# A fused cross-attention kernel: the sum of squares folded over two partition halves, one matmul per norm, output products reordered

## The chip, the cores and the metric

The kernel runs on one core of one Trainium2 chip. Time is device time in microseconds of one execution; the profiled execution has its own time and, in its trace, a span from the first to the last instruction. TensorE (PE in the rows) multiplies, VectorE (DVE), ScalarE (ACT) and GpSimd (POOL) work elementwise, SyncE (SP) issues most of the DMAs. Each runs its instructions in order, and they wait for each other through semaphores.

## What is computed

One cross-attention layer over 64 sequences of 256 tokens, in float32. The text input x has 512 features, the context 384, the hidden size is 512. Cut to its core:

```python
text_p = einsum('bld,dh->blh', H_l, W_text) + b_text
audio_p = einsum('bsd,dh->bsh', H_a, W_audio) + b_audio
Q = layer_norm(text_p, g1, beta1)
K = layer_norm(audio_p, g2, beta2)
alpha = softmax(einsum('blh,bsh->bls', Q, K) / sqrt(512))
H_hyper = einsum('bls,bsh->blh', alpha, audio_p)
H_hyper = einsum('blh,hk->blk', H_hyper, W_out) + b_out
out = layer_norm(H_hyper + H_l, g_out, beta_out)
```

## The kernel before

**Steps.** A step handles two sequences, 512 tokens, and there are N = 32 of them. The first two and the last two are written out, the others run in a loop of two steps a turn (run_steps). In step i the projections, the norms and the scores of step i are made, together with the probabilities, the context product and the output product of step j = i - 1, and the last norm of the rows of step i - 2.

**Two-part numbers.** The operands of TensorE are written in type fp32r, in two parts: a high part, and a low part that holds what is left of the float32 value. Each product is three matmuls: high by high, high by low, low by high. The high part is a copy on ScalarE, as a rule, and the low part a subtraction on VectorE (low, shifted_low).

**K and Q.** project_k and project_q give four tiles each (h = 0 to 3) of 128 hidden features by 512 tokens, into the PSUM banks wide0 to wide3. The mean over the features is already taken out, through centred weights. k_centre and q_centre on ScalarE read a tile twice: its square goes to squares[:, h, :], the tile itself to k_cols or q_cols. The variance is the mean of squares over all 512 features: POOL adds tiles 0 and 1 (pair_squares), VectorE adds tile 2 (add_square) and tile 3 (sum_squares), splits the 128x512 sum into sq_hi and sq_lo (split_sum), and mean_squares on TensorE multiplies each by a constant 128x128 matrix of 1/512 (mean_of), two matmuls into one bank, turn0 for k and turn1 for q. The bank then holds the variance of each token in all 128 rows. rstd_of on ScalarE (Ln, then Exp) turns it into 1/sqrt in place, k_norm or q_norm on VectorE multiplies each tile by it, k_high or q_high on ScalarE and k_low or q_low on VectorE split the result. The scores need kT and qT in both parts. scores waits for one qT tile per term: qT_split counts them, and the first product, scores(0, 0), waits for all four, one before each term of three matmuls.

**The rest of a step.** turn_p turns the probabilities of step j with transposes of 32 rows on VectorE, sixteen a step (512 in all), twelve ahead of the k sum and four behind it. pT_high and pT_low split them. probs_context(j, d) makes the context product in three blocks d = 0, 1, 2 into score[0], score[1] and turn0; pc_high and pc_low split each, and output_part(j, t, d) multiplies block d with the folded output weights into wide[t]: three matmuls for each of four row tiles t and three blocks d, 36 a step. y_sum adds the rows, y_stat and y_moment give the statistics, scales on POOL the factors, y_norm on ScalarE normalises, and finish_y on POOL multiplies by go_row and adds betao_row (lines 963 and 965).

**What sets the order.** There is no scheduler. The order on each engine is the order of the calls in its step function. The ones that the change touches: on TensorE mean_squares(k) stands between project_q(1) and project_q(2), and mean_squares(q) between probs_context(j, 2) and the output products. On VectorE the k sum stands behind twelve transposes. On ScalarE q_centre(0) follows y_norm(i - 2, odd, 0); xT_high(i + 1), a 128x2048 copy, stands between q_high(1) and q_high(2).

Of the kernel before, what the change touches and what calls it, by code (L numbers as in the profile page):

```python
# [14 lines left out]
P = 128  # L15
# [3 lines left out]
def cross_attention_kernel(nc, x_rows, xT, c_rows, cT, w_text, b_text, w_audio, b_audio, w_out, b_out,  # L19
# [11 lines left out]
    with ExitStack() as stack:  # L31
# [39 lines left out]
        sq_hi, sq_lo = sb("sq_hi", [P, T * P], F32R), sb("sq_lo", [P, T * P], F32R)  # L71
# [51 lines left out]
        mean_of_made = sem("mean_of_made")  # L123
        k_log, q_log, k_rstd, q_rstd = sem("k_log"), sem("q_log"), sem("k_rstd"), sem("q_rstd")
# [7 lines left out]
        k_added, k_summed, k_sq_hi, k_sq_lo = sem("k_added"), sem("k_summed"), sem("k_sq_hi"), sem("k_sq_lo")  # L132
        q_added, q_summed, q_sq_hi, q_sq_lo = sem("q_added"), sem("q_summed"), sem("q_sq_hi"), sem("q_sq_lo")
# [117 lines left out]
        def _(pe):  # L251
# [48 lines left out]
            def mean_squares(i, to, sq_hi_made, sq_lo_made, var):  # L300

                pe.wait_ge(sq_hi_made, i + 1)
                nc.tensor.matmul(to, mean_of[:], sq_hi[:], start=True, stop=False)
                pe.wait_ge(sq_lo_made, i + 1)
                nc.tensor.matmul(to, mean_of[:], sq_lo[:], start=False, stop=True).then_inc(var, 1)  # L305
# [73 lines left out]
            def step(i, odd, first=False, last=False):  # L379
# [5 lines left out]
                mean_squares(i, turn[0][:], k_sq_hi, k_sq_lo, k_var)  # L385
# [12 lines left out]
                mean_squares(i, turn[1][:], q_sq_hi, q_sq_lo, q_var)  # L398
                if not first:

                    pe.wait_ge(q_centred, HT * i + 2)
                    output_part(j, 0, 0)
                    output_part(j, 0, 1)
                    output_part(j, 1, 0)
                if not first:
                    output_part(j, 0, 2)
                    output_part(j, 1, 1)
                    output_part(j, 1, 2)
                    for t in range(2, T - 1 if last else T):
                        pe.wait_ge(q_centred, HT * i + t + 1)  # L410
                        output(j, t)
# [26 lines left out]
        def _(act):  # L438
# [37 lines left out]
            def k_centre(i, h):  # L476
                wait(act, kT_split, HT * (i - 1) + h + 1)
                wait(act, q_sq_lo if h == 3 else q_summed, i)
                centre(k_cols, h, bac_col, k_done, i, k_centred, k_squared)

            def q_centre(i, h):
                wait(act, qT_split, HT * (i - 1) + h + 1)
                act.wait_ge(k_sq_lo if h == 3 else k_summed, i + 1)
                centre(q_cols, h, btc_col, q_done, i, q_centred, q_squared)

# [62 lines left out]
            def step(i, odd, first=False, last=False):  # L548
# [13 lines left out]
                k_centre(i, 3)  # L562
                if late:
                    y_norm(i - 2, odd, 0)
# [11 lines left out]
                q_centre(i, 3)  # L576
                k_high(i, 3)
# [3 lines left out]
                else:  # L581
                    for d in range(CT):
# [491 lines left out]
```

## Time and profile before

| what | value |
|---|---|
| median of 3 runs | 1299.43 us (1299.04 to 1299.71) |
| profiled execution: its time | 1299.89 us |
| its span | 1298.1 us |
| mean granted TensorE clock | 0.992 of full speed |
| TensorE busy | 98% |
| VectorE busy | 1164.0 us, 90% |
| ScalarE busy | 1001.5 us, 77% |
| POOL busy | 724.4 us, 56% |

Busy shares are of the whole span. A matmul is listed with its own time from start to drained result (395 ns for 512 columns), while the next one starts sooner; what a matmul costs is the distance between two starts. Times in a timeline are counted from the start of the span, so one can place what one engine does beside another. The text in square brackets behind a row is the idle time ahead of it and whose result ended it.

### The profile page before, as it was taken

The page shows a single profiled execution, that of the slowest core. Times are in us where ns is not written, and L with a number is a line of the kernel's source. Part 1 is how long each engine was busy: PE and PEld are TensorE (multiplying, and loading weights), DVE is VectorE, ACT ScalarE, POOL GpSimd, SP SyncE. Part 2 cuts the span into 40 slices and gives each one's busy share as a digit, 9 for nine tenths or more (in the row PEclk, how much of TensorE's full clock was granted, in tenths as well). Part 3 has the DMA queues.
Part 4 walks back from the last instruction along what each step waited for, and adds up shares of the span by engine and source line. Part 5 has one row for each costly group of instructions (what it writes and reads, how often), then busy time and mean ns, then how long its engine had stood idle before and what let it go on. Part 6 is the DMA issues. An engine that isn't in the chain of part 4 may idle for free.

```text
span 1298.1 us, 22641 instructions
## 1 busy us (share of the span) xinstructions
PE 1270.3 (98%) x6704; PEld 1077.7 (83%) x6704; DVE 1164.0 (90%) x2049; ACT 1001.5 (77%) x1655; POOL 724.4 (56%) x757
## 2 busy tenths in 40 slices
PE   7999999999999999999999999999999999999994
PEld 5688888888888888888888888888888888888874
DVE  5689999999999999998999999999998999899987
ACT  6677787887787887787887787887787887787862
POOL 1123666555666555666555666555666555665564
PEclk9999999999999999999999999999999999999997
DMA  7454755566755566755566755666755566755662
GB/s 251 130 119 126 203 174 144 157 188 186 202 183 122 171 187 186 202 173 143 157 189 186 202 179 124 170 189 186 202 174 142 157 190 186 202 182 118 176 175 79
DMA packets 76693, 221.02 MB, mean 170 GB/s; under 512 B 9856, under 2 KB 9856, under 8 KB 68480
## 3 DMA queue, kind: packets, MB, share of 16 engines
q1 hardware_dynamic: 55312, 154.70, 33.7%
q0 software_dynamic: 21360, 66.06, 26.7%
q8 instruction: 10, 0.16, 0.0%
q14 instruction: 11, 0.09, 0.0%
HBM read 121.12 MB, written 33.55 MB: 119 GB/s over the span
## 4 chain that ended last, share of the span: by engine, by line
PE 94%; DVE 3%; ACT 1%; DMA 1%; issue 1%; SPq 1%; DVEq 0%; ACTq 0%
PE wide L294 9%; PE wide L296 9%; PE wide L295 9%; PE scores_both L261 7%; PE scores_both L262 7%; PE scores_both L263 7%; PE wide L341 7%; PE wide L343 7%; PE wide L342 7%; PE wide L263 7%; PE wide L261 7%; PE wide L262 6%; PE turn L305 1%; PE turn L262 1%; PE turn L261 1%; PE turn L263 1%
## 5 line engine op out<-in xcount | busy, mean ns | idle before, releaser
L963 POOL TENSOR_TENSOR y_rows<-y_rows,go_row 128x512 f32<-128x512 f32 x120 | 156.4, 1304 | 216.3 <-ACT y_rows L505 216.3
L658 DVE STREAM_TRANSPOSE scores_both<-probs 32x256 f32<-32x256 f32 x512 | 233.4, 456 | 8.2 <-ACT probs L514 0.2
L294 PE MATMUL wide<-xT_hi,wt_hi 128*128 128x512 f32 x512 | 202.1, 395 | 0.8 <-ACT k_cols L474 0.8
L296 PE MATMUL wide<-xT_hi,wt_lo 128*128 128x512 f32 x512 | 202.1, 395 | 0.0
L295 PE MATMUL wide<-xT_lo,wt_hi 128*128 128x512 f32 x512 | 201.8, 394 | 0.0
L943 POOL DMA_DIRECT2D xT_lo<-xT_in x31 | 27.9, 899 | 248.1 <-ACT xT_lo L447 248.1
L965 POOL TENSOR_TENSOR y_rows<-y_rows,betao_row 128x512 f32<-128x512 f32 x120 | 155.7, 1297 | 9.4
L473 ACT ACTIVATE squares<-wide,bac_col 128x512 f32<-128x512 f32 x128 | 88.2, 689 | 90.3 <-PE wide L263 90.3
L341 PE MATMUL wide<-wao_hi,pcT_hi 128*128 128x512 f32 x384 | 153.4, 400 | 0.0
L261 PE MATMUL wide<-cT_hi,wa_hi 128*128 128x512 f32 x384 | 152.3, 397 | 0.3 <-DVE wa_lo L782 0.3
L263 PE MATMUL wide<-cT_hi,wa_lo 128*128 128x512 f32 x384 | 152.2, 396 | 0.0
L262 PE MATMUL wide<-cT_lo,wa_hi 128*128 128x512 f32 x384 | 152.0, 396 | 0.0
L343 PE MATMUL wide<-wao_hi,pcT_lo 128*128 128x512 f32 x384 | 151.6, 395 | 0.0
L342 PE MATMUL wide<-wao_lo,pcT_hi 128*128 128x512 f32 x384 | 151.4, 394 | 0.0
L261 PE MATMUL scores_both<-kT_hi,qT_hi 128*128 128x256 f32 x512 | 145.5, 284 | 1.0 <-DVE qT_lo L705 1.0
L263 PE MATMUL scores_both<-kT_hi,qT_lo 128*128 128x256 f32 x512 | 144.8, 283 | 0.0
L262 PE MATMUL scores_both<-kT_lo,qT_hi 128*128 128x256 f32 x512 | 144.8, 283 | 0.0
L705 DVE SCALAR_TENSOR_TENSOR qT_lo<-q_cols,beta_col,qT_hi 128x512 fp32r<-128x512 f32 x128 | 123.8, 969 | 8.9 <-ACT qT_hi L500 0.7
L949 POOL TENSOR_TENSOR c_lo<-c_kept,c_hi 128x384 fp32r<-128x384 f32 x128 | 127.9, 1076 | 4.7 <-ACT c_hi L452 4.7
L500 ACT ACTIVATE qT_hi<-q_cols,beta_col 128x512 fp32r<-128x512 f32 x128 | 90.4, 724 | 48.3 <-DVE q_cols L699 47.8
L505 ACT ACTIVATE y_rows<-y_rows,y_sc 128x512 f32<-128x512 f32 x120 | 94.3, 810 | 42.5 <-POOL y_sc L932 42.5
L699 DVE SCALAR_TENSOR_TENSOR k_cols<-k_cols,g_col,turn 128x512 f32<-128x512 f32 x128 | 92.2, 742 | 31.1 <-ACT turn L491 31.0
(120 smaller groups left out, 3570.4 us busy)
## 6 DMA issues: line engine op xcount, KB each, us to landing
xT_in<-in_xT SPq DMA_DIRECT2D x32, 1024.0 KB, 9.6
y_rows<-in_x_rows SPq DMA_DIRECT2D x124, 256.0 KB, 4.4
xT_lo<-xT_in POOLq DMA_DIRECT2D x31, 1024.0 KB, 7.0
y_rows<-bao_row POOLq DMA_DIRECT2D x31, 1024.0 KB, 10.4
out<-y_rows SPq DMA_DIRECT2D x124, 256.0 KB, 2.3
cT_in<-in_cT SPq DMA_DIRECT2D x32, 768.0 KB, 7.7
c_kept<-in_c_rows SPq DMA_DIRECT2D x32, 768.0 KB, 6.8
q_cols<-in_L_xattn_W_text SPq DMA_DIRECT2D x1, 1024.0 KB, 5.8
```

Source lines behind the costliest of these rows:

```text
L261: nc.tensor.matmul(to, a_hi, b_hi, start=(m == 0), stop=False)
L262: nc.tensor.matmul(to, a_hi, b_lo, start=False, stop=False)
L263: done = nc.tensor.matmul(to, a_lo, b_hi, start=False, stop=(m == n - 1))
L294: nc.tensor.matmul(wide[h][:], wt_hi[:, d, cols], xT_hi[:, d, :], start=(d == 0), stop=False)
L295: nc.tensor.matmul(wide[h][:], wt_hi[:, d, cols], xT_lo[:, d, :], start=False, stop=False)
L296: done = nc.tensor.matmul(wide[h][:], wt_lo[:, d, cols], xT_hi[:, d, :], start=False, stop=(d == DT - 1))
L341: nc.tensor.matmul(wide[t][:], hi, wao_hi[:, d, :], start=(d == 0), stop=False)
L342: nc.tensor.matmul(wide[t][:], hi, wao_lo[:, d, :], start=False, stop=False)
L343: done = nc.tensor.matmul(wide[t][:], lo, wao_hi[:, d, :], start=False, stop=(d == CT - 1))
L658: done = nc.vector.transpose(to[Q * b:Q * (b + 1), :, Q * a:Q * (a + 1)], of[Q * a:Q * (a + 1), :, Q * b:Q * (b + 1)])
L963: nc.gpsimd.tensor_tensor(rows, rows, go_row[:], ALU.mult).then_inc(y_scaled, 1)
L965: nc.gpsimd.tensor_tensor(rows, rows, betao_row[:], ALU.add).then_inc(y_ready, 1)
```

## The change

**Folding.** The 128x512 sum of squares is folded to 64 rows before it is split, so that the high part fits into rows 0 to 63 and the low part into rows 64 to 127 of one operand, sq_parts. ScalarE first copies rows 64 to 127 of the sum into the PSUM bank that is free at that time (move_half, into turn0 or turn1), and VectorE adds that to rows 0 to 63 (halve_sum, giving sq_half). split_sum then writes both parts on 64 rows each, and mean_squares is one matmul instead of two. The variance is the same sum.

**Order.** On TensorE, output products are made block by block: block 0 of tiles 0 and 1, then mean_squares(q), block 0 of the other tiles, then blocks 1 and 2 tile by tile. On ScalarE move_half(k) stands behind k_centre(3) and waits for the k sum, and move_half(q) stands behind pc_high(0), which moves ahead of k_high(3). On VectorE pc_low(0) moves between the q sum and the fold, k_low(1) behind the split, and pc_low(1), k_low(2), pc_low(2), k_low(3) follow in turn. The transposes stay as they are.

```diff
-                mean_squares(i, turn[0][:], k_sq_hi, k_sq_lo, k_var)
+                mean_squares(i, turn[0][:], k_sq_parts, k_var)
                 project_q(i, 2)
                 project_q(i, 3)
...
-                mean_squares(i, turn[1][:], q_sq_hi, q_sq_lo, q_var)
-                if not first:
-
+                tiles = range(T - 1 if last else T)
+                if not first:
                     pe.wait_ge(q_centred, HT * i + 2)
                     output_part(j, 0, 0)
-                    output_part(j, 0, 1)
                     output_part(j, 1, 0)
-                if not first:
-                    output_part(j, 0, 2)
-                    output_part(j, 1, 1)
-                    output_part(j, 1, 2)
-                    for t in range(2, T - 1 if last else T):
+                mean_squares(i, turn[1][:], q_sq_parts, q_var)
+                if not first:
+                    for t in tiles[2:]:
                         pe.wait_ge(q_centred, HT * i + t + 1)
-                        output(j, t)
+                        output_part(j, t, 0)
+                    for t in tiles:
+                        output_part(j, t, 1)
+                        output_part(j, t, 2)
...
+            def move_half(i, to, summed, moved):
+
+                act.wait_ge(summed, i + 1)
+                nc.scalar.copy(to[P // 2:P, :], squares[P // 2:P, 3, :]).then_inc(moved, 1)
...
                 k_centre(i, 3)
+                move_half(i, turn[0], k_summed, k_moved)
                 if late:
                     y_norm(i - 2, odd, 0)
                 q_centre(i, 0)
...
                 q_centre(i, 3)
+                if not first:
+                    pc_high(j, 0)
+                move_half(i, turn[1], q_summed, q_moved)
                 k_high(i, 3)
...
-            def split_sum(i, var_before, before, summed, hi_made, lo_made):
+            def halve_sum(i, of, moved, halved):
+
+                dve.wait_ge(moved, i + 1)
+                nc.vector.tensor_tensor(sq_half[:], squares[0:P // 2, 3, :], of[P // 2:P, :],
+                                        ALU.add).then_inc(halved, 1)
+
+            def split_sum(i, var_before, before, halved, hi_made, parts_made):
 
                 wait(dve, var_before, before)
-                dve.wait_ge(summed, i + 1)
-                nc.vector.tensor_copy(sq_hi[:], squares[:, 3, :]).then_inc(hi_made, 1)
+                dve.wait_ge(halved, i + 1)
+                nc.vector.tensor_copy(sq_parts[0:P // 2, :], sq_half[:]).then_inc(hi_made, 1)
                 dve.wait_ge(hi_made, i + 1)
-                low(sq_lo[:], squares[:, 3, :], sq_hi[:]).then_inc(lo_made, 1)
+                low(sq_parts[P // 2:P, :], sq_half[:], sq_parts[0:P // 2, :]).then_inc(parts_made, 1)
...
                 sum_squares(i, k_squared, k_added, k_summed)
-                split_sum(i, q_var, i, k_summed, k_sq_hi, k_sq_lo)
+                halve_sum(i, turn[0], k_moved, k_halved)
+                split_sum(i, q_var, i, k_halved, k_sq_hi, k_sq_parts)
```

**VectorE, the k sum.** Behind the twelve transposes; before, with the four transposes that follow the split:

```order
L676 TENSOR_TENSOR squares<-squares 128x512
L682 REGISTER_ALU
L683 TENSOR_TENSOR squares<-squares 128x512
L690 CAST sq_hi<-squares 128x512
L640 TENSOR_TENSOR sq_lo<-squares,sq_hi 128x512
L658 STREAM_TRANSPOSE scores_both<-probs 32x8x32 x4
```

and in the changed kernel:

```order
L684 TENSOR_TENSOR squares<-squares 128x512
L690 REGISTER_ALU
L691 TENSOR_TENSOR squares<-squares 128x512
L697 TENSOR_TENSOR sq_half<-squares,turn 64x512
L704 CAST sq_parts<-sq_half 64x512
L648 TENSOR_TENSOR sq_parts<-sq_half,sq_parts 64x512
L666 STREAM_TRANSPOSE scores_both<-probs 32x8x32 x4
```

One add of 64 rows stands between the sum and the split; its second input comes from the bank turn, which ScalarE fills.

**VectorE, the q sum.** Before, from add_square to the last kT_lo:

```order
L676 TENSOR_TENSOR squares<-squares 128x512
L705 SCALAR_TENSOR_TENSOR kT_lo<-k_cols,beta_col,kT_hi 128x512
L683 TENSOR_TENSOR squares<-squares 128x512
L690 CAST sq_hi<-squares 128x512
L640 TENSOR_TENSOR sq_lo<-squares,sq_hi 128x512
L668 ISA
L640 TENSOR_TENSOR pcT_lo<-scores_both,pcT_hi 128x512
L668 REGISTER_ALU
L640 TENSOR_TENSOR pcT_lo<-scores_both,pcT_hi 128x512
L705 SCALAR_TENSOR_TENSOR kT_lo<-k_cols,beta_col,kT_hi 128x512
```

and in the changed kernel:

```order
L684 TENSOR_TENSOR squares<-squares 128x512
L691 TENSOR_TENSOR squares<-squares 128x512
L676 ISA
L648 TENSOR_TENSOR pcT_lo<-scores_both,pcT_hi 128x512
L697 TENSOR_TENSOR sq_half<-squares,turn 64x512
L704 CAST sq_parts<-sq_half 64x512
L648 TENSOR_TENSOR sq_parts<-sq_half,sq_parts 64x512
L719 SCALAR_TENSOR_TENSOR kT_lo<-k_cols,beta_col,kT_hi 128x512
L676 REGISTER_ALU
L648 TENSOR_TENSOR pcT_lo<-scores_both,pcT_hi 128x512
```

The first pcT_lo now stands between the sum and the fold, and the second kT_lo, which stood between the two adds of squares, comes behind the split.

**TensorE, between the context product and the output products.** Before:

```order
L263 MATMUL turn<-pT_hi,c_lo 128x256
L303 MATMUL turn<-sq_hi,mean_of 128x512
L305 MATMUL turn<-sq_lo,mean_of 128x512
L341 MATMUL wide<-wao_hi,pcT_hi 128x512
L342 MATMUL wide<-wao_lo,pcT_hi 128x512
```

and in the changed kernel:

```order
L265 MATMUL turn<-pT_hi,c_lo 128x256
L341 MATMUL wide<-wao_hi,pcT_hi 128x512
L342 MATMUL wide<-wao_lo,pcT_hi 128x512
L343 MATMUL wide<-wao_hi,pcT_lo 128x512
L341 MATMUL wide<-wao_hi,pcT_hi 128x512
L342 MATMUL wide<-wao_lo,pcT_hi 128x512
L343 MATMUL wide<-wao_hi,pcT_lo 128x512
L305 MATMUL turn<-sq_parts,mean_of 128x512
```

The two matmuls on the sum have become one, and it stands behind six output matmuls. (In these lists the matmul's names are target, moving operand, stationary operand.)

## Rows read from the trace of the kernel before

**Rows 1.** The page's line of busy time, share and instructions of each engine.

```profile
PE 1270.3 (98%) x6704; PEld 1077.7 (83%) x6704; DVE 1164.0 (90%) x2049; ACT 1001.5 (77%) x1655; POOL 724.4 (56%) x757
```

**Rows 2.** Who waited for whom: us in total, times, longest.

```profile
PE scores_both L261 <- DVE qT_lo L705: 1.0, 2, 0.7
```

**Rows 3.** Timeline, TensorE, one step: start us, duration us, engine, line, operation.

```profile
600.43 0.39 PE L261 MATMUL wide<-cT_hi,wa_hi 128*128 128x512 f32 x1
...
614.37 0.40 PE L303 MATMUL turn<-sq_hi,mean_of 128*128 128x512 f32 x1
614.60 0.40 PE L305 MATMUL turn<-sq_lo,mean_of 128*128 128x512 f32 x1
...
624.95 0.40 PE L305 MATMUL turn<-sq_lo,mean_of 128*128 128x512 f32 x1
625.18 0.42 PE L341 MATMUL wide<-wao_hi,pcT_hi 128*128 128x512 f32 x1
...
626.61 0.39 PE L341 MATMUL wide<-wao_hi,pcT_hi 128*128 128x512 f32 x1
...
634.65 0.28 PE L261 MATMUL scores_both<-kT_hi,qT_hi 128*128 128x256 f32 x1
...
639.33 0.39 PE L261 MATMUL wide<-cT_hi,wa_hi 128*128 128x512 f32 x1
```

**Rows 4.** Timeline, VectorE, same step; xN: N in a row merged.

```profile
611.58 0.69 DVE L683 TENSOR_TENSOR squares<-squares 128x512 f32<-128x512 f32 x1
...
612.84 0.69 DVE L640 TENSOR_TENSOR sq_lo<-squares,sq_hi 128x512 fp32r<-128x512 f32 x1
613.57 1.87 DVE L658 STREAM_TRANSPOSE scores_both<-probs 32x256 f32<-32x256 f32 x4
616.44 1.41 DVE L699 SCALAR_TENSOR_TENSOR k_cols<-k_cols,g_col,turn 128x512 f32<-128x512 f32 x2 [0.99 <-ACT turn L491]
...
627.42 1.40 DVE L699 SCALAR_TENSOR_TENSOR q_cols<-q_cols,g_col,turn 128x512 f32<-128x512 f32 x2
628.95 1.76 DVE L705 SCALAR_TENSOR_TENSOR qT_lo<-q_cols,beta_col,qT_hi 128x512 fp32r<-128x512 f32 x1
...
631.29 0.74 DVE L705 SCALAR_TENSOR_TENSOR qT_lo<-q_cols,beta_col,qT_hi 128x512 fp32r<-128x512 f32 x1
...
632.61 1.63 DVE L705 SCALAR_TENSOR_TENSOR qT_lo<-q_cols,beta_col,qT_hi 128x512 fp32r<-128x512 f32 x2
```

**Rows 5.** Timeline, ScalarE, same step.

```profile
611.70 0.82 ACT L505 ACTIVATE y_rows<-y_rows,y_sc 128x512 f32<-128x512 f32 x1 [1.44 <-POOL y_sc L932]
...
615.73 0.58 ACT L491 ACTIVATE turn<-turn 128x512 f32<-128x512 f32 x1
...
617.36 0.59 ACT L462 CAST pT_hi<-scores_both 128x512 fp32r<-128x512 f32 x1
...
623.05 1.12 ACT L468 CAST pcT_hi<-scores_both 128x512 fp32r<-128x512 f32 x2
...
626.59 0.81 ACT L505 ACTIVATE y_rows<-y_rows,y_sc 128x512 f32<-128x512 f32 x1
```

**Rows 6.** Timeline, POOL, same step: the products behind y_norm(1).

```profile
627.49 1.29 POOL L963 TENSOR_TENSOR y_rows<-y_rows,go_row 128x512 f32<-128x512 f32 x1 [7.37 <-ACT y_rows L505]
628.86 1.30 POOL L965 TENSOR_TENSOR y_rows<-y_rows,betao_row 128x512 f32<-128x512 f32 x1
```

**Rows 7.** Timeline, TensorE, last step: the fourth term of the first scores.

```profile
1257.40 0.39 PE L261 MATMUL scores_both<-kT_hi,qT_hi 128*128 128x256 f32 x1 [0.26 <-DVE qT_lo L705]
1257.63 0.28 PE L262 MATMUL scores_both<-kT_lo,qT_hi 128*128 128x256 f32 x1
```

**Rows 8.** Timeline, VectorE, last step: qT_lo(2) and qT_lo(3).

```profile
1255.73 1.62 DVE L705 SCALAR_TENSOR_TENSOR qT_lo<-q_cols,beta_col,qT_hi 128x512 fp32r<-128x512 f32 x2
```

**Rows 9.** Timeline, VectorE, step 2: the k sum.

```profile
104.06 1.57 DVE L683 TENSOR_TENSOR squares<-squares 128x512 f32<-128x512 f32 x1
```

**Rows 10.** Busy us per engine in a stretch; the third number from the end is PEclk.

```profile
1217.00:1256.00 39.00, 38.74 (x210) 32.99 (x208) 35.80 (x64) 29.42 (x51) 24.34 (x25) 1.00 0.73 182
```

More of the change, by code:

```diff
@@ L123, in cross_attention_kernel @@
         mean_of_made = sem("mean_of_made")
+        k_moved, q_moved = sem("k_moved"), sem("q_moved")
         k_log, q_log, k_rstd, q_rstd = sem("k_log"), sem("q_log"), sem("k_rstd"), sem("q_rstd")
@@ L131, in cross_attention_kernel @@
         xT_split, cT_split, pT_split, pc_split = sem("xT_split"), sem("cT_split"), sem("pT_split"), sem("pc_split")
-        k_added, k_summed, k_sq_hi, k_sq_lo = sem("k_added"), sem("k_summed"), sem("k_sq_hi"), sem("k_sq_lo")
-        q_added, q_summed, q_sq_hi, q_sq_lo = sem("q_added"), sem("q_summed"), sem("q_sq_hi"), sem("q_sq_lo")
+        k_added, k_summed, k_halved = sem("k_added"), sem("k_summed"), sem("k_halved")
+        q_added, q_summed, q_halved = sem("q_added"), sem("q_summed"), sem("q_halved")
+        k_sq_hi, k_sq_parts, q_sq_hi, q_sq_parts = sem("k_sq_hi"), sem("k_sq_parts"), sem("q_sq_hi"), sem("q_sq_parts")
         k_normed, q_normed = sem("k_normed"), sem("q_normed")
@@ L298, in project_q, with mean_squares @@
                     done.then_inc(q_done, 1)
[L300 to L305, printed above, removed]
+            def mean_squares(i, to, parts_made, var):
+                pe.wait_ge(parts_made, i + 1)
+                nc.tensor.matmul(to, mean_of[:], sq_parts[:], start=True, stop=True).then_inc(var, 1)
             def scores(i, b, l):
@@ L477, in k_centre @@
                 wait(act, kT_split, HT * (i - 1) + h + 1)
-                wait(act, q_sq_lo if h == 3 else q_summed, i)
+                wait(act, q_halved if h == 3 else q_summed, i)
                 centre(k_cols, h, bac_col, k_done, i, k_centred, k_squared)
@@ L581, in step @@
                 else:
-                    for d in range(CT):
-                        pc_high(j, d)
+                    pc_high(j, 1)
+                    pc_high(j, 2)
                 rstd_of(i, turn[1], q_var, q_log, q_rstd)
@@ L836, in step @@
                 add_square(i, q_paired, q_squared, q_added)
-                k_low(i, 1)
                 sum_squares(i, q_squared, q_added, q_summed)
-                split_sum(i, k_var, i + 1, q_summed, q_sq_hi, q_sq_lo)
                 if not first:
                     pc_low(j, 0)
+                halve_sum(i, turn[1], q_moved, q_halved)
+                split_sum(i, k_var, i + 1, q_halved, q_sq_hi, q_sq_parts)
+                k_low(i, 1)
+                if not first:
                     pc_low(j, 1)
@@ L845, in step @@
                     pc_low(j, 2)
-                k_low(i, 3)
                 if first:
@@ L849, in step @@
                     wao_low(1)
+                k_low(i, 3)
                 q_norm(i, 0)
```

4 lines of the change are left out of this document (2 added, 2 removed).

## The prediction

> **What bounds the kernel now.** I read the busy table first: TensorE is busy 98% of the span, VectorE 90% [rows 1]. Then TensorE's waits: what it waits for most within the steps is qT_lo, with 1.0 us in all, twice, so hardly ever [rows 2]. So a matmul saved in the loop is time saved, as long as nothing that TensorE waits for gets later. How near the others are is in the timelines of one step in the middle. TensorE starts it at 600.43 and the next at 639.33: 38.90 us [rows 3]. In that step two things reach TensorE with little to spare:
> - the split k sum: its low part ends at 613.53 (612.84 + 0.69), its matmul starts at 614.60 [rows 3, 4];
> - qT_lo(3), for the fourth term of the first scores: it ends at 634.24 (632.61 + 1.63 for two), the matmul starts at 634.65 [rows 3, 4].
>
> What TensorE needs between VectorE's end and a matmul is seen in the last step, where it does stall on qT_lo: VectorE ends at 1257.35 (1255.73 + 1.62), the matmul is listed at 1257.40, and the next one at 1257.63, where running ones are 0.12 apart, so the restart is worth 0.16 us (1257.63 - 0.12 - 1257.35) [rows 7, 8]. The slack of qT_lo(3) is then 634.65 - 634.24 - 0.16 = **0.25 us**. That stall also shows that this wait is the next one in line: it appears as soon as TensorE arrives earlier (in the last step it skips nine output matmuls).
>
> **What the change takes away.** One matmul of 512 columns per norm. Spacing is the price, not the listed 0.40 us: L303 at 614.37, L305 at 614.60, so 0.23 us, twice a step, 0.47 us a step and 64 x 0.23 = 14.9 us in all. The output products are only reordered: 36 a step as before.
>
> **The k half.** VectorE's sum ends at 612.27 (611.58 + 0.69) [rows 4]. Before, cast and low followed and ended at 613.53. Now:
> 1. ScalarE's copy into turn0 has no row. The nearest is the 128x512 PSUM cast at 0.59 us; bounds are 0.30 (half of it, if time went with partitions) and 0.82 (y_norm, the same columns from SBUF) [rows 5]. I take 0.59, since a column of all partitions moves at once here: the transposes work on 32 partitions and 256 columns and take 1.87 / 4 = 0.47 us [rows 4], no quarter of a full one. ScalarE is free: it stood 1.44 us waiting for POOL until 611.70, and now the copy goes ahead of y_norm(0). Its start is 0.04 behind the sum, 612.31 to 612.90; y_norm(0) and q_centre(0) behind it end 0.7 us later, still before the Ln.
> 2. halve_sum, a 512-column add: 0.69 as the sum, 612.94 to 613.63. Bounds 0.35 (if time went with partitions) and 0.82.
> 3. cast after a 0.11 hand-over and low, as before: 613.74 to 614.17, 614.20 to 614.89. That is 1.36 us later than 613.53.
>
> TensorE comes to this matmul at 614.37 and can begin at 614.89 + 0.16 = 615.05. It stalls 0.68 us, saves 0.23, and everything behind is 0.45 later. So is the Exp of the k norm, which ended at 616.31 [rows 5]. On VectorE the four transposes of the last quadrant slide from 613.57 to 614.93 and end at 616.80; its 0.99 us of waiting for turn shrinks to about 0.1 and swallows the rest [rows 4]. k_norm(0) starts 0.45 late. With both lower bounds low ends at 614.26, TensorE hardly stalls and all of this is 0.18 us earlier instead; with both upper ones it is 0.81 later.
>
> **The q half, TensorE's side.** mean_squares(q) is moved behind six output matmuls, which take 626.61 - 625.18 = 1.43 us [rows 3]. Its last matmul began at 624.95, its first 0.23 before that, at 624.72; the single one now begins at 624.72 + 0.45 + 1.43 = 626.60, which is **1.65 us later**. Ln, Exp and y_norm(1) on ScalarE follow it back to back (y_norm(1) at 626.59), and POOL's two row products follow y_norm(1) (627.49 and 628.86) [rows 5, 6]. All of them move by 1.65: POOL's second ends at 631.81 instead of 630.16.
>
> **The q half, VectorE's side.** add_square ran right behind k_norm(3), whose place moves by 0.45, so it now ends at about 622.3; the sum, without k_low(1) between, runs to 623.1 or 623.2. pc_high(0), at 623.05 before [rows 5], goes ahead of k_high(3) (0.6 us) and stands 0.45 later: 622.9 to 623.44; the copy behind it 623.37 to 623.96; on VectorE pc_low(0) 623.48 to 624.17, halve_sum to 624.87, cast and low to 626.13; with 0.16 that is 0.31 before TensorE asks. Then k_low(1), pc_low(1), k_low(2), pc_low(2), k_low(3) at 0.66 and 0.61 each: 3.2 us, q_norm(0) at 629.3 instead of 627.42, **+1.9 us**. Of this 0.45 is the k half, 0.61 the new add, the rest the hand-overs that had other work in them.
>
> **Where the two sides meet.** q_low(0) takes 1.76 us in this step where q_low(1) takes 0.74 [rows 4]. It began at 628.95, just behind POOL's second product (628.86), and ended 0.55 us after that one's end [rows 6]. The row shows it held by POOL. In the changed kernel it would begin at 628.95 + 1.9 = 630.85, while POOL's product runs 630.51 to 631.81: held again, end at 632.36, 1.65 later than 630.71. The spacings behind it stay, ScalarE's qT_hi(3) is not late, and qT_lo(3) ends at 634.24 + 1.65 = 635.89. TensorE restarts at 636.05, then needs 639.33 - 634.65 = 4.68 us to the end of the step, and ends at 640.73. **A step takes 40.30 us instead of 38.90, 1.40 more** (shift 1.65 less slack 0.25). TensorE's idle per step is 0.68 + 1.19 us.
>
> By the Trainium skill (SBUF — State Buffer, Who interferes with whom) a VectorE instruction with two SBUF inputs and a GpSimd instruction that reads SBUF shut each other out for whole instructions, by which starts first. Rows 4 and 6 agree, 1.76 against 0.74 us. By it the new add, with one input in PSUM, would not be held.
>
> By the Trainium skill (VectorE: DVE Perf Modes, Two Vector instructions with no wait between them) an instruction whose output starts in another quadrant of partitions than the last begins only when all before it are done. The rows show only its other side: two q_norm take 1.40 us, less than two q_low(1) of 0.74, so unheld ones overlap by some 0.07. It speaks against the change, which writes the low part from partition 64 and reads turn from there: some 0.2 us more ahead of q_low(0), hidden under POOL's hold, and a little less chance that the hold is missed.
>
> **The sum, against the profiled run (span 1298.1, time 1299.89; the median of the runs is 0.46 lower).** Steps 3 to 30: 28 x 1.40 = 39.2. Step 2: before, POOL's products caught the k sum and the cast there (1.57 us instead of 0.69 for the sum) [rows 9]; now they are gated by the later y_norm(0) and would catch cast and low; I put 1.0 on top of the 1.40 for the step. Step 0 has no transposes to hide behind and no matmul to spare at the k sum, step 1 has no POOL hold: 1.0 each. Last step: no slack to give, 1.65. After the loop nothing changes. Together 45.3: 1345.2 on the profiled run, and **1345 us** as a median.
>
> **The rivals.**
> - *The hold is missed.* VectorE reaches q_low(0) before POOL's second product and is through at 631.6. Then ScalarE sets the end: xT_high stands between qT_hi(1) and qT_hi(2), qT_hi(3) ends at 634.7 and qT_lo(3) at 635.45, shift 1.2. Step +0.96: 28 x 0.96 + 6 gives 1333. Against it: by my times q_low(0) starts 0.34 us behind POOL. 13%.
> - *A hold in the k chain at every step.* POOL's first product of y_rows, behind y_norm(0), catches cast or low as it caught the sum in step 2 [rows 9]. One such product takes 1.29 us [rows 6], so up to 1.3 more a step: 1345 + 28 x 1.3 = 1381. Against: beyond step 2 POOL still has its four scales to do at that time, and cast and low, not it, come first. 6%.
> - *Only instruction time counts.* If the hand-overs were covered, VectorE's lengthening is 2 x 0.61 - 0.99 = 0.23, the slack 0.25: the step stays 38.9, 1299. 4%.
> - *Faster: VectorE absorbs it.* The deciding number is how late qT_lo(3) comes. Up to 0.25 us late the step is no longer than now; at 0 it is 0.25 shorter (31 x 0.25 = 8 us, 1291); for the whole 0.47 a step, 1299.4 - 14.9 = 1285, it must even come 0.22 earlier. For it speaks that TensorE has 98% and VectorE 10% idle. Against it: VectorE gets 64 adds of 0.69, 44 us, and the idle time that lies ahead of qT_lo(3) in a step is the 0.99 before k_norm [rows 4]; what lies behind the scores cannot be pulled ahead. 9%, at 1288.
>
> The forecast has 68%, with 1338 to 1352 as its own range (0.2 us either way a step, from the bounds of copy and add; step 2). At the lower bounds of copy and add the q half shifts by 1.43 - 0.23 - 0.18 = 1.0, a step +0.77, 1299.4 + 28 x 0.77 + 5 = 1326. At the upper ones it is +1.76 a step, 1355. The range for 8 in 10 takes in both and the missed hold: 1322 to 1360. Within 0.2% is what a measurement of this kernel can tell from no change. Faster 9%, same 4%, slower 87%.
>
> **What the profile will show.** Right: about 30 waits of TensorE on the low part of the k sum at 0.5 to 0.9 us (PE or PEld, on turn), and some 30 on qT_lo totalling about 1.2 a step; VectorE 1209 us busy (1164 + 44); the wait of k_norm for turn nearly gone; q_low(0) still near 1.6; ScalarE's new COPY near 0.59. The granted clock stays at its full level (2.4 GHz), as in the last step, where TensorE stalled on qT_lo and the stretch before has 1.00 [rows 10]. Wrong: if TensorE has no waits on VectorE in the loop, or if q_norm(0) follows mean_squares(q) directly, so that TensorE's order and not VectorE's load sets the q half; then the 1.43 us of moved output products is the whole cause.

## The result, and the profile after

| | before | after |
|---|---|---|
| median of the runs | 1299.24 us (1298.71 to 1299.71) | 1354.49 us (1353.39 to 1355.84) |
| profiled execution: time, span | 1299.89, 1298.1 us | 1354.41, 1352.6 us |
| one step in the middle | 38.9 us | 40.7 us |

The changed kernel is **slower**: ratio 1.0426, 95% interval 1.0408 to 1.0444. The forecast was 1345 us, with 1322 to 1360 as its range. Direction and mechanism held; the time came out 9.5 us above the point and 2.5 above the forecast's own range of 1338 to 1352, inside the wide one. The first line below answers to [rows 1]: TensorE went from 98% to 95% of the span, VectorE from 1164.0 to 1216.8 us. The second is the chain that ended last, by engine.

```profile
PE 1285.3 (95%) x6640; PEld 1068.2 (79%) x6640; DVE 1216.8 (90%) x2113; ACT 1043.9 (77%) x1719; POOL 733.9 (54%) x757
...
DVE 45%; ACT 22%; PE 18%; issue 13%; DMA 1%; SPq 1%; DVEq 0%; ACTq 0%; POOL 0%
```

Who waited for whom in the changed kernel (us in total, times, longest) answers to [rows 2]. TensorE, which hardly waited in the loop, now stalls at two places in each step: on the low part of a sum of squares (sq_parts), and on qT_lo. A third, smaller wait, for pcT_lo, shows on the weight load's side (14.6 us, 35 times). The wait of k_norm for turn, 31.0 us in all before, is 1.9.

```profile
PE scores_both L263 <- DVE qT_lo L719: 24.0, 61, 0.7
...
PE turn L305 <- DVE sq_parts L648: 16.5, 32, 1.5
```

**One step in the middle**, on four engines. It starts on TensorE at 624.66 and the next one at 665.34, so 40.68 us. First VectorE, the k half and the q half, to be held against [rows 4]:

```profile
635.81 0.71 DVE L691 TENSOR_TENSOR squares<-squares 128x512 f32<-128x512 f32 x1
637.17 0.69 DVE L697 TENSOR_TENSOR sq_half<-squares,turn 64x512 f32<-64x512 f32 x1 [0.65 <-ACT turn L488]
637.98 0.42 DVE L704 CAST sq_parts<-sq_half 64x512 fp32r<-64x512 f32 x1
638.43 0.72 DVE L648 TENSOR_TENSOR sq_parts<-sq_half,sq_parts 64x512 fp32r<-64x512 f32 x1
...
641.15 1.41 DVE L713 SCALAR_TENSOR_TENSOR k_cols<-k_cols,g_col,turn 128x512 f32<-128x512 f32 x2
...
650.51 0.75 DVE L719 SCALAR_TENSOR_TENSOR kT_lo<-k_cols,beta_col,kT_hi 128x512 fp32r<-128x512 f32 x1
651.29 0.69 DVE L648 TENSOR_TENSOR pcT_lo<-scores_both,pcT_hi 128x512 fp32r<-128x512 f32 x1
651.90 0.74 DVE L719 SCALAR_TENSOR_TENSOR kT_lo<-k_cols,beta_col,kT_hi 128x512 fp32r<-128x512 f32 x1
...
653.16 0.74 DVE L719 SCALAR_TENSOR_TENSOR kT_lo<-k_cols,beta_col,kT_hi 128x512 fp32r<-128x512 f32 x1
653.82 1.40 DVE L713 SCALAR_TENSOR_TENSOR q_cols<-q_cols,g_col,turn 128x512 f32<-128x512 f32 x2
655.36 1.64 DVE L719 SCALAR_TENSOR_TENSOR qT_lo<-q_cols,beta_col,qT_hi 128x512 fp32r<-128x512 f32 x1
...
658.89 1.62 DVE L719 SCALAR_TENSOR_TENSOR qT_lo<-q_cols,beta_col,qT_hi 128x512 fp32r<-128x512 f32 x2
```

TensorE in the same step, against [rows 3]: the two single matmuls of the norms, and the first scores, which it enters by pieces because each waits for a head of qT_lo.

```profile
639.20 0.50 PE L305 MATMUL turn<-sq_parts,mean_of 128*128 128x512 f32 x1 [0.44 <-DVE sq_parts L648]
...
650.82 0.39 PE L305 MATMUL turn<-sq_parts,mean_of 128*128 128x512 f32 x1
...
659.69 0.39 PE L263 MATMUL scores_both<-kT_hi,qT_hi 128*128 128x256 f32 x1 [0.53 <-DVE qT_lo L719]
...
660.57 0.39 PE L263 MATMUL scores_both<-kT_hi,qT_hi 128*128 128x256 f32 x1 [0.26 <-DVE qT_lo L719]
```

ScalarE's copy and the Exp of the k norm ([rows 5]), then POOL's two products behind y_norm(1) ([rows 6]):

```profile
636.55 0.59 ACT L488 COPY turn<-squares 64x512 f32<-64x512 f32 x1 [2.06 <-DVE squares L691]
...
640.44 0.58 ACT L495 ACTIVATE turn<-turn 128x512 f32<-128x512 f32 x1
```

```profile
653.33 1.72 POOL L980 TENSOR_TENSOR y_rows<-y_rows,go_row 128x512 f32<-128x512 f32 x1 [8.79 <-ACT y_rows L509]
655.13 1.31 POOL L982 TENSOR_TENSOR y_rows<-y_rows,betao_row 128x512 f32<-128x512 f32 x1
```

The first of them takes 1.72 us, where it took 1.29 before. Nothing in the forecast had that; more of it below.

**Where the 54.5 us are.** Cut at the second neg_max of each step, the two traces differ by 0.9 up to step 0, 1.0 in step 1, 1.5 in step 2 (40.09 to 41.60), 48.6 in steps 3 to 30 (1090.55 to 1139.11, so 1.73 a step), 3.3 in the last step (38.85 to 42.19), and -0.9 behind the loop.

### The profile page after: what moved, and what is told of

It reads as the page before. It is cut to its first block, busy times and chain, and to the rows that moved or that the text cites. A ratio compares the mean times of both kernels' runs of the same rounds, so it can differ in the third digit from the quotient of the medians.

```text
span 1352.6 us, 22641 instructions
## 1 busy us (share of the span) xinstructions
PE 1285.3 (95%) x6640; PEld 1068.2 (79%) x6640; DVE 1216.8 (90%) x2113; ACT 1043.9 (77%) x1719; POOL 733.9 (54%) x757
## 4 chain that ended last, share of the span: by engine, by line
DVE 45%; ACT 22%; PE 18%; issue 13%; DMA 1%; SPq 1%; DVEq 0%; ACTq 0%; POOL 0%
DVE scores_both L666 12%; DVE qT_lo L719 7%; DVE pcT_lo L648 5%; DVE q_cols L713 4%; PE scores_both L263 4%; ACT squares L472 4%; PE scores_both L265 4%; PE scores_both L264 4%; ACT q_cols L473 4%; ACT qT_hi L504 3%; DVE sq_half L697 3%; DVE kT_lo L719 3%; ACT pT_hi L461 2%; DVE sq_parts L648 2%; DVE sq_parts L704 2%
## 5 line engine op out<-in xcount | busy, mean ns | idle before, releaser
L980 POOL TENSOR_TENSOR y_rows<-y_rows,go_row 128x512 f32<-128x512 f32 x120 | 169.2, 1410 | 259.0 <-ACT y_rows L509 259.0
L263 PE MATMUL scores_both<-kT_hi,qT_hi 128*128 128x256 f32 x512 | 152.4, 298 | 24.2 <-DVE qT_lo L719 24.0
L263 PEld LDWEIGHTS scores_both<-kT_hi,qT_hi 128*128 128x128 f32 x512 | 98.2, 192 | 39.2 <-DVE qT_lo L719 37.0
L296 PEld LDWEIGHTS wide<-xT_hi,wt_hi 128*128 128x128 f32 x512 | 96.5, 188 | 22.7 <-ACT k_cols L473 1.4
```

The lines of the kernel that those rows point to most:

```text
L263: nc.tensor.matmul(to, a_hi, b_hi, start=(m == 0), stop=False)
L296: nc.tensor.matmul(wide[h][:], wt_hi[:, d, cols], xT_hi[:, d, :], start=(d == 0), stop=False)
L980: nc.gpsimd.tensor_tensor(rows, rows, go_row[:], ALU.mult).then_inc(y_scaled, 1)
```

## The experiments

Every ratio is to the kernel before in the same series of runs (1298.97 to 1299.08 us). The edits are shown in part; "..." stands for what is left out.

### The two halves, one at a time

fold_k_only folds the sum of the k norm alone, and keeps the old order on TensorE and on the q side. fold_q_only folds the sum of the q norm alone, with the new order; its edit against the changed kernel:

```diff
-                mean_squares(i, turn[0][:], k_sq_parts, k_var)
+                mean_squares_two(i, turn[0][:], k_sq_hi, k_sq_parts, k_var)
...
-                move_half(i, turn[0], k_summed, k_moved)
...
-                halve_sum(i, turn[0], k_moved, k_halved)
-                split_sum(i, q_var, i, k_halved, k_sq_hi, k_sq_parts)
+                split_two(i, q_var, i, k_summed, k_sq_hi, k_sq_parts)
```

Both keep the halved sum in a part of squares, so two of ScalarE's squares (k_centre(2), q_centre(2)) have to wait for the split. Between 100 and 1250 us ScalarE's squares wait for VectorE only once, 2.2 us, in fold_q_only, and not at all in fold_k_only, so this extra condition costs next to nothing.

> Only the k norm is folded; the q norm has its two matmuls, and TensorE, VectorE and ScalarE their old order in the q half. Theory: the k half alone costs TensorE's stall of about 0.7 less the 0.23 of the matmul, 0.45 a step, and nothing is added at the scores: 1313 us (1309 to 1317). Rival (the stall at the k sum is absorbed by slack further on): 1299 or less.

> Only the q norm is folded, with the changed order of the q half; the k norm is as before. Theory: the rest, 1.3 us a step, 1340 us, so that the two halves add up to the whole (14 + 41 of 55); if q_low(0) escapes POOL's second product, about 1326. Rival (the halves need each other): less than 1315.

Measured: k alone **1314.01 us** (ratio 1.0114, 1.0098 to 1.0131), q alone **1337.17** (1.0292, 1.0275 to 1.0309). They add 15.0 and 38.2, together 53.2 of the 55.3. So each half has its own price, as the forecast had it: its k half was 0.45 a step, 14 us; the k fold alone lengthens a step by 0.42 (39.37 against 38.95, the means of steps 3 to 30).

### The order without the fold, and the fold without the order

order_only has TensorE's new order and nothing else. fold_old_order is the changed kernel with TensorE's old order.

```diff
-                mean_squares(i, turn[1][:], q_sq_hi, q_sq_lo, q_var)
-                if not first:
-
+                tiles = range(T - 1 if last else T)
+                if not first:
                     pe.wait_ge(q_centred, HT * i + 2)
                     output_part(j, 0, 0)
-                    output_part(j, 0, 1)
                     output_part(j, 1, 0)
...
+                mean_squares(i, turn[1][:], q_sq_hi, q_sq_lo, q_var)
...
```

> The kernel before, with only TensorE's new order of output products (block by block, mean_squares(q), still two matmuls, behind six of them). Theory (VectorE's longer chain is the cause, the order only carries a hold along): the q norm's Ln and Exp come 1.4 us later, q_norm(0) 0.8 later, q_low(0) is due during POOL's first product and gets in between the two, about 0.2 us late, inside the slack of 0.25: 1299 to 1303 us. Rival (the moved output products are the cause): q_low(0) waits for POOL's second product as well, everything 1.4 us late, a step 1.2 longer: 1335 or more.

> The changed kernel with TensorE's output products in the old order, mean_squares(q) right behind the context product. Theory: TensorE comes to mean_squares(q) 1.5 us before the low part is there and stalls there instead of at the scores; VectorE's chain is the same, so 1342 to 1358 us. Rival (the order is the cause): the 1.4 us of a step come back, about 1310 to 1320.

Neither the theory nor the rival of either run held. order_only took **1317.93 us** (1.0145, 1.0128 to 1.0162), 19 above before, and fold_old_order **1367.69** (1.0528, 1.051 to 1.0545), 13 above the changed kernel. In order_only TensorE meets an output product that now stands ahead of the norm, while its pcT_lo still stands behind the split on VectorE:

```profile
633.45 0.47 PE L341 MATMUL wide<-wao_hi,pcT_hi 128*128 128x512 f32 x1 [0.25 <-DVE pcT_lo L639]
```

In fold_old_order the wait for qT_lo is nearly gone (1.3 us, 3 times) and TensorE stands at both sums instead, twice as often as in the changed kernel, and once a step on pcT_lo (9.6 us in all):

```profile
PE turn L305 <- DVE sq_parts L649: 45.6, 63, 1.5
```

That left open whether the later norm or the wait on pcT_lo makes the new order dear. all_order_no_fold has the order of the changed kernel on all engines (pc_high(0) and pc_low(0) ahead, k_low(1) behind the split), and no fold: two matmuls, no copy, no halving.

```diff
-                halve_sum(i, turn[1], q_moved, q_halved)
-                split_sum(i, k_var, i + 1, q_halved, q_sq_hi, q_sq_parts)
+                split_two(i, k_var, i + 1, q_summed, q_sq_hi, q_sq_parts)
                 k_low(i, 1)
...
```

The k side is changed in the same way.

> The order of the changed kernel on all engines (TensorE's output products by context block, ScalarE's pc_high(0) and VectorE's pc_low(0) ahead of the split of the sum of q, k_low(1) behind it), but without the fold: sum of squares split over all 128 partitions, two matmuls for each norm, no copy, no halving. With TensorE's new order alone the time was 1317.9 us, step 39.55, with a wait of 0.28 us a step of an output product on pcT_lo of block 0. Theory: half of that cost was this wait, which goes when pc_low(0) stands early; what is left is that the norm of q comes behind two output products more, so that Ln, Exp and q_norm come some 1.1 to 1.4 us later and q_low(0) runs into GpSimd's products: step 39.2 to 39.3, time 1309 us (1304 to 1313). Rival A: the wait on pcT_lo was all of it: 1299 to 1303 us. Rival B: the later norm was all of it, or pc_low(0) ahead of the split only moves the wait to the norm: 1316 to 1321 us.

Measured: **1302.53 us** (1.0024, 1.0014 to 1.0034), step 39.02. My theory, 1309, is wrong and its rival A is right: the order of the moves on VectorE and ScalarE, with pc_low(0) and pc_high(0) early, was most of it, 15.4 of 18.9 us. The run moves these two and k_low(1) together, so it doesn't show how much each is worth. The norm that comes two outputs later costs at most 3.4, and of these 1.7 are the last step alone (40.50 against 38.85). There TensorE's granted clock falls, as it does in the changed kernel (last section): 18 matmuls of the scores are 0.21 apart instead of 0.12, which is some 1.6 us. So on its own the reordering costs 3.4 us and **the fold costs 52.0** (1354.5 - 1302.5), while with the fold in place the new order of TensorE saves 13.2: it lays six output products over the sum of q.

### What the fold is made of: the copy and the hold

no_copy has no copy on ScalarE; the fold adds rows 0 to 63 of another tile, so the sum is another number. Both inputs of that add then lie in SBUF; it took 0.67 us, so nothing held it. hold_gone shortens POOL's two products of finish_y(1) to one column. no_copy_no_hold does both.

```diff
-                act.wait_ge(summed, i + 1)
-                nc.scalar.copy(to[P // 2:P, :], squares[P // 2:P, 3, :]).then_inc(moved, 1)
+                pass
```

```diff
-                nc.gpsimd.tensor_tensor(rows, rows, go_row[:], ALU.mult).then_inc(y_scaled, 1)
+                nc.gpsimd.tensor_tensor(rows, rows, go_row[:, 0:n], ALU.mult).then_inc(y_scaled, 1)
```

> The changed kernel without ScalarE's copy: the fold adds rows 0 to 63 of another tile of squares instead, so the variance leaves half of the features out and takes others twice. Work of VectorE and TensorE is the same, the round trip to ScalarE is gone. Theory: 0.6 us less at the k sum, TensorE's stall there falls to about 0.1, everything behind is 0.6 earlier: a step 40.1 us, 1336 us (1328 to 1342). Rival (the add itself and not the round trip is what costs): 1350 or more.

> The changed kernel, with POOL's two products of row tile 1 (finish_y(1), the ones behind y_norm(1)) cut to one column of 512; the rest of that tile is left unmultiplied. Theory (POOL holds q_low(0)): q_low(0) falls from 1.63 to 0.74 us, then ScalarE's xT_high is next, qT_lo(3) comes 0.6 us earlier: a step 40.1 us, 1336 us (1330 to 1341). Rival (q_low(0) is long for another reason, or its length does not matter): 1354.

> The changed kernel without ScalarE's copy of a half (the fold adds rows 0 to 63 of another tile of squares, so the sum is a wrong one) and with the two products of finish_y(1) on one column instead of 512 (so a quarter of the output isn't scaled and shifted). Alone, the first took 27.3 us off the changed kernel and the second 20.9 us. Theory: the copy lengthens the way to the norms and the hold by GpSimd lengthens the way from the norm of q to the scores; both lie on one path in turn, so the gains add up: step 40.67 - 0.87 - 0.64 = 39.16 us, time 1306 us (1300 to 1312). Rival: both edits shorten the same wait (without the copy the q side is early enough to slip past GpSimd's products), then little is left for the second: 1320 to 1327 us.

Measured: no_copy **1327.15** (1.0216, 1.0199 to 1.0233), hold_gone **1333.64** (1.0267, 1.025 to 1.0284), both together **1306.63** (1.0058, 1.0042 to 1.0075). Off the changed kernel that is 27.3, 20.9 and 47.9: they add up, so they lie one behind the other on one path. What is left is 4.1 us above all_order_no_fold: the two adds and what they make late use up the two matmuls saved in each step, and 4.1 us more. Without the hold q_low(0) takes 0.75 us, on VectorE in hold_gone:

```profile
645.10 1.40 DVE L713 SCALAR_TENSOR_TENSOR q_cols<-q_cols,g_col,turn 128x512 f32<-128x512 f32 x2
646.63 0.75 DVE L719 SCALAR_TENSOR_TENSOR qT_lo<-q_cols,beta_col,qT_hi 128x512 fp32r<-128x512 f32 x1
```

no_copy came out 9 us better than I had written, just below its range. In it POOL's first product takes 1.47 instead of 1.72 us: VectorE's kT_lo(3) is through sooner and lies over less of it. That was the first sign of the next point.

```profile
640.35 1.47 POOL L979 TENSOR_TENSOR y_rows<-y_rows,go_row 128x512 f32<-128x512 f32 x1 [7.57 <-ACT y_rows L508]
```

### The residual: who holds whom

In the changed kernel kT_lo(3) runs from 653.16 to 653.90, and POOL's product starts at 653.33. low_first exchanges one pair of moves on VectorE, so that pc_low(2), with one of its inputs in PSUM, lies there instead.

```diff
                 k_low(i, 2)
+                k_low(i, 3)
                 if not first:
                     pc_low(j, 2)
...
-                k_low(i, 3)
                 q_norm(i, 0)
```

> The changed kernel with one pair of VectorE's moves exchanged: the last low part of k (kT_lo of head 3) stands ahead of the last low part of the product probabilities x context (pcT_lo of block 2). In the changed kernel that kT_lo takes 0.74 us and lies over the start of GpSimd's first product of finish_y(1), which takes 1.72 us there and 1.29 us before. Theory: that product is held by VectorE's kT_lo for 0.4 us a step, the second product and the held q_low(0) behind it end 0.4 us later, and this is the part of the 40.67 us step that the sum of the prediction (40.30) did not have. Expected: first product 1.3 us, step 40.25 to 40.35, time 1343 us (1340 to 1347). Rival: the 1.72 us are the product's own spread, or pcT_lo holds it as well; then the step stays at 40.67 and the time at 1354 us (1352 to 1356).

Measured: **1340.0 us** (1.0315, 1.0298 to 1.0332), step 40.24, as the theory had it, at the lower end of its range. Timeline of low_first, VectorE and then POOL:

```profile
647.47 0.68 DVE L648 TENSOR_TENSOR pcT_lo<-turn,pcT_hi 128x512 fp32r<-128x512 f32 x1
648.07 1.40 DVE L713 SCALAR_TENSOR_TENSOR q_cols<-q_cols,g_col,turn 128x512 f32<-128x512 f32 x2
649.60 1.17 DVE L719 SCALAR_TENSOR_TENSOR qT_lo<-q_cols,beta_col,qT_hi 128x512 fp32r<-128x512 f32 x1
```

```profile
647.58 1.27 POOL L980 TENSOR_TENSOR y_rows<-y_rows,go_row 128x512 f32<-128x512 f32 x1 [8.79 <-ACT y_rows L509]
648.92 1.30 POOL L982 TENSOR_TENSOR y_rows<-y_rows,betao_row 128x512 f32<-128x512 f32 x1
```

POOL's product starts 0.11 us behind the start of pcT_lo and takes 1.27. So the hold goes both ways: in the changed kernel VectorE held POOL for 0.4 us, and POOL then held q_low(0) by as much longer (1.64 against 1.17 here, where it is still held for 0.4). By the Trainium skill (SBUF — State Buffer, Who interferes with whom) a VectorE instruction with two SBUF inputs and a GpSimd one that reads SBUF exclude each other, and the one that issues first goes first. The rows agree, 1.72 against 1.27 us; I had used it for one direction only.

The exchange has a price of its own, since it makes block 2 of pcT_lo later. TensorE's stall moves there, away from qT_lo:

```profile
PE wide L341 <- DVE pcT_lo L648: 20.7, 31, 1.0
...
648.21 0.50 PE L341 MATMUL wide<-wao_hi,pcT_hi 128*128 128x512 f32 x1 [0.66 <-DVE pcT_lo L648]
...
654.36 0.39 PE L263 MATMUL scores_both<-kT_hi,qT_hi 128*128 128x256 f32 x1
```

The last line is the fourth term of the first scores, 0.19 behind the matmul before it instead of 0.12. So qT_lo(3), which ends 35.41 us into the step, still decides the step's length, by a hair. Of the 14.5 us that the exchange gave back, 12.3 are in steps 3 to 30; some 1.4 are in the last step, where TensorE's clock no longer falls.

### TensorE's side alone

high_only is the kernel before with the high part of the sum alone: one matmul for each norm and no subtraction, so the mean of squares lacks its low part. high_no_cast also lets VectorE write the sum in the rounded type, without a cast.

```diff
                 pe.wait_ge(sq_hi_made, i + 1)
-                nc.tensor.matmul(to, mean_of[:], sq_hi[:], start=True, stop=False)
-                pe.wait_ge(sq_lo_made, i + 1)
-                nc.tensor.matmul(to, mean_of[:], sq_lo[:], start=False, stop=True).then_inc(var, 1)
+                nc.tensor.matmul(to, mean_of[:], sq_hi[:], start=True, stop=True).then_inc(var, 1)
```

> The kernel before with the high part of the sum alone in mean_squares: one matmul per norm, no low part on VectorE, no fold; the variance leaves out what the high part's rounding leaves. Theory (TensorE is the bound and a matmul is worth its spacing, as long as VectorE's chain does not grow): 64 x 0.233 = 14.9 us less, 1284.5 us (1283 to 1287). Rival (qT_lo sets the step as soon as TensorE is 0.25 us faster, hold by POOL included): 1291 or more.

> The kernel before with the high part of the sum of squares only and one matmul for each norm (time 1281.6 us, step 38.43 us, the low part is left out), and now also without the cast: VectorE's last addition writes the sum into the rounded type directly, one instruction of 0.47 us less on VectorE for each norm and about 0.5 us less on the way to each norm. Theory: at 38.43 us a step TensorE has no wait left for VectorE, so neither VectorE's time nor a shorter way to the norms gives anything: 1281.6 us (1280.5 to 1282.5), same within 0.1 %. Rival: the way to the norms still ends waits somewhere in a step, then up to 2 x 0.5 us a step come off: 1265 to 1275 us.

Measured: **1281.64 us** (0.9865, 0.9849 to 0.9881) and **1280.74** (0.9857, 0.9841 to 0.9873). The first is 1.4 us below the range that I had given it (1283 to 1287). Its steps are 38.43 us as a rule, exactly the 38.90 less two spacings of 0.23; steps 3 to 30 give 28 x 0.52 = 14.6 us (the mean before was 38.948), step 2 gives 1.3 (38.81 against 40.09), the last step 1.2. What the range had left out is what is gained beyond two spacings a step: 1.5 us in steps 3 to 30, 0.8 in step 2 and 0.8 in the last. The second frees VectorE of 28 us of casts (its busy time goes from 1114.8 to 1086.9) and gets 0.9 us for it, in intervals that overlap: with TensorE as the bound, a shorter way to the norm is worth nothing. Both beat the kernel before, at the price of the low part; whether that precision can be spared is not for these runs to say.

### y_norm(1) out of the way

norm_later moves y_norm(1) on ScalarE behind the last q_high, so that POOL's products come behind q_low.

```diff
-                if late:
-                    y_norm(i - 2, odd, 1)
                 q_high(i, 0)
...
                 q_high(i, 3)
+                if late:
+                    y_norm(i - 2, odd, 1)
```

> The changed kernel with y_norm(1) on ScalarE moved behind q_high(3), so that POOL's two products come behind q_low(0), beside cT_low and y_sum. Nothing is left out. Theory: the hold of q_low(0) is gone, one hold of a cT_low comes instead, which has the idle time ahead of the second neg_max to fall into: 1338 us (1331 to 1345). Rival (the new hold costs as much): 1354.

Measured: **1455.2 us** (1.1221, 1.1171 to 1.1271), far from both. The four executions spread from 1444.0 to 1462.5; the one in the trace took 1444.0. q_low(0) is free, at 0.75 us, but the products are late and come in one row with POOL's other work, and the whole row falls on VectorE's cT_lo, on which TensorE waits six matmuls into the next step. VectorE, POOL and TensorE of one step:

```profile
615.54 5.66 DVE L648 TENSOR_TENSOR cT_lo<-cT_in,cT_hi 128x512 fp32r<-128x512 f32 x1
```

```profile
615.49 3.94 POOL L966 TENSOR_TENSOR c_lo<-c_kept,c_hi 128x384 fp32r<-128x384 f32 x4
619.34 1.31 POOL L980 TENSOR_TENSOR y_rows<-y_rows,go_row 128x512 f32<-128x512 f32 x1
```

```profile
621.26 0.80 PE L263 MATMUL wide<-cT_hi,wa_hi 128*128 128x512 f32 x1 [4.07 <-DVE cT_lo L648]
```

So cT_lo stood through five POOL instructions in a row and ended 0.55 us behind the last. Hiding the hold by a later y_norm only moves it to a place where TensorE pays all of it.

## Why the prediction held, and where it was off

Times in brackets are from the step's start on TensorE: forecast, then measured.

- **What bounds it, and the direction.** Right. TensorE stalls where the forecast had it: 32 times on a sum's low part (16.5 us, 0.52 each) and on qT_lo 61 times (24.0 us, 0.77 a step, and 37.0 on the weight load's side, 1.2 a step). These waits are counted from the drained result of the matmul before. Counted by starts, as the forecast's 0.68 and 1.19 are, the matmul behind the k norm comes 0.71 late in the step above, and the scores take 1.30 longer (7.06 us, before 5.76).
- **A matmul is worth 0.23.** Right, where nothing else gets later: high_only, which also spares VectorE the subtraction, shortens the step from 38.90 to 38.43, 0.47.
- **The k half.** Right throughout. The copy took 0.59 and the add 0.69, both on 64 partitions; sq_parts low ended at 14.49 (14.46), Exp at 16.36 (16.33), k_norm(0) began at 16.49 (16.46), and its wait for turn went from 31.0 to 1.9 us. Half the partitions saved nothing: the durations of the 128-partition rows, 0.59 and 0.69, were the right choice between the bounds.
- **The q half on TensorE and ScalarE.** Right: mean_squares(q) at 26.16 (26.17), POOL's first product at 28.67 (28.71).
- **The q half on VectorE.** q_norm(0) came 0.3 later, 29.16 (28.87). Part of that is the hold on quadrants that the forecast left out of its sum: in the rows above kT_lo and the pcT_lo behind it, just after the split, are 0.78 apart where the forecast had 0.66. By the Trainium skill (VectorE: DVE Perf Modes, Two Vector instructions with no wait between them) an instruction whose input in a memory starts in another quadrant than the last one read there waits for all before it; pcT_lo reads PSUM from partition 0 behind the read of turn from 64, and the row agrees; in no_copy, where the add reads no PSUM, the same two are 0.67 apart. Another 0.12 was there when the split ended, at 25.82 (25.70): the sum before it, which waits 0.27 for ScalarE's square, ended 0.1 to 0.2 later than forecast. All of it was hidden under POOL's hold, as said.
- **Where the two sides meet: the step that failed.** That q_low(0) is held was right, 1.64 us (1.6). That POOL's second product ends 1.65 later was not: it took for granted that the first lasts 1.29 again, and it lasted 1.72, held by kT_lo(3). q_low(0) ended at 32.34 (31.93), qT_lo(3) at 35.85 (35.46), and the step took 40.68 instead of 40.30. This is a term of the sum that was too small, 39.2 for steps 3 to 30 where 48.6 came, by a cause that low_first shows: without it qT_lo(3) ends at 35.41, the step is 40.24 and the time 1340. That is 5 us under the forecast, so the rest of the sum was too high by that much (1.4 in step 2, 0.9 behind the loop, and 0.1 in each of the 28 steps), and some luck lies in how near 1345 came to 1354.
- **The small terms.** Steps 0 and 1: 0.9 and 1.0 (1.0 each). Step 2: 1.5, not 2.4; POOL caught one instruction, the low part at 1.65 us, not cast and low. Last step: 3.3, not 1.65. Of the difference 0.4 is the residual; the rest is TensorE's clock, below: in low_first, where the clock stays up, the last step is 1.5 longer than before. Behind the loop -0.9 where nothing was put.
- **VectorE's busy time.** 1216.8 us, not 1209. The 64 adds are 44.2 of the 52.8; the other 8.6 I put down to overlaps of neighbours that are lost where one is held; that is argued and not shown.
- **The rivals.** The hold was not missed; what its absence is worth was priced well, 1333 against the 1333.64 us of hold_gone. A hold in the k chain came in step 2 alone. The "faster" case asked that qT_lo(3) be no later; it is 2.0 later in the step (35.85, before 33.81). The last sentence of the forecast, that the moved output products might be the whole cause, is refuted by all_order_no_fold: 3.4 us. They do take part: they put POOL's products 1.43 later, and q_low(0) ends when these let it go. But in all_order_no_fold, without the fold, q_low(0) comes earlier and gets in between the two products (1.07 us).
- **The granted clock** was to stay at its full level. It did in the steady steps, and not in the last one; that cost some 1.4 us, which no term of the sum had.

## What to carry to other kernels

A matmul saved is worth its spacing only as long as what feeds the next one is no later; a fold that puts a copy, an add and two hand-overs between sum and matmul costs here some 67 us (an estimate, 52.0 + 14.9) to save 14.9. Count an operation on half the partitions at its full price. Where two engines exclude each other, write down both starts and ask both ways who holds whom: exchanging one pair of moves with the same work gave 14.5 us back here. Then look at what the moved work itself makes wait.

## What the runs showed of the hardware that I had not expected

**TensorE's clock falls after stalls that are short.** In the last step of the changed kernel, TensorE waits three times for qT_lo, is busy 1.83 of 3.40 us, and the granted clock in the next 3.2 us is 0.51, its 1.2 GHz level; the stretches before and after are at 1.00. Busy time of each engine by stretch, the third number from the end is the granted clock:

```profile
1300.00:1308.00 8.00, 7.51 (x32) 5.26 (x32) 7.67 (x12) 4.42 (x8) 3.03 (x2) 1.00 1.02 173
1308.00:1311.40 3.40, 1.83 (x9) 1.23 (x9) 3.27 (x6) 2.25 (x3) 0.00 (x0) 0.96 0.21 80
1311.40:1314.60 3.20, 3.17 (x15) 3.17 (x16) 1.30 (x2) 1.98 (x3) 2.56 (x3) 0.51 0.01 3
1314.60:1320.00 5.40, 5.19 (x35) 4.46 (x34) 4.52 (x10) 2.46 (x10) 5.24 (x6) 1.00 0.09 34
```

There the matmuls of the scores are 0.21 apart instead of 0.12, so 15 of them cost 1.4 us more: with the 0.4 of the residual that is the last step's 3.3 against 1.65. In the last step of the kernel before, two waits are listed, 0.70 and 0.26 us, and the clock stays at 1.00:

```profile
1250.00:1257.00 7.00, 6.22 (x30) 4.87 (x28) 6.74 (x9) 3.79 (x6) 2.59 (x2) 1.00 0.91 176
1257.00:1261.00 4.00, 3.74 (x32) 3.60 (x31) 3.17 (x6) 3.13 (x6) 2.99 (x4) 1.00 0.02 6
```

In the changed kernel a wait of 0.64 us comes ahead of these two. fold_q_only and no_copy have the same three waits, all_order_no_fold has 0.48, 0.70 and 0.26, and in all three the matmuls go to a spacing of 0.21. order_only, with 0.46, 0.70 and 0.26, and fold_old_order, with 0.33, 0.70 and 0.26, keep 0.12. So the number of waits alone doesn't decide it; what does is not shown. In two steady stretches, with stalls of 0.26 to 0.53 us that stand apart, it stays at 1.00 (the first two lines below, of the changed kernel). In norm_later, behind the stall of 4.07 us, it is 0.55 (the line by itself).

```profile
600.00:639.00 39.00, 38.00 (x201) 31.75 (x199) 35.71 (x62) 31.35 (x52) 21.84 (x23) 1.00 0.60 172
639.00:678.00 39.00, 38.01 (x201) 32.16 (x202) 35.72 (x64) 30.66 (x52) 21.99 (x22) 1.00 0.58 159
```

```profile
620.00:627.00 7.00, 5.74 (x15) 4.59 (x16) 6.67 (x15) 3.57 (x11) 4.78 (x4) 0.55 0.33 101
```

**A hold can last through several instructions.** In norm_later one VectorE instruction, 0.68 us where it is free, took 5.66 us, through five POOL instructions that followed one another without a gap.
